# An attention and gated-FFN block on one core: half-row FFN tiles, two down banks, two work banks, and scores kept in PSUM

## Time and profile before

| | |
|---|---|
| median of 3 runs | 1118.66 us (1116.5 to 1118.77) |
| the profiled execution's own time | 1114.17 us |
| its span | 1112.0 us |
| PE, DVE, ACT, POOL busy | 84%, 80%, 54%, 63% |
| mean granted TensorE clock | 0.943 of full |

### The profile page before, as it was taken

The page is one execution under the profiler, slowest core; times in us unless marked ns, Lnnn a source line. Parts: engine busy times, 40 slices in busy tenths (PEclk is TensorE's granted clock), DMA queues, the critical chain, the costliest instruction groups (busy, mean ns, idle before and its releaser), DMA issues.

```text
span 1112.0 us, 13901 instructions
## 1 busy us (share of the span) xinstructions
PE 932.1 (84%) x4423; PEld 511.2 (46%) x4423; DVE 890.0 (80%) x1135; ACT 603.9 (54%) x907; POOL 697.9 (63%) x497
## 2 busy tenths in 40 slices
PE   5633538999889988999899988999899979889995
PEld 4432424555445544554445545454455543434442
DVE  4999997899798988899789988899889989642213
ACT  2546646655385646756475747655565635523422
POOL 2556555777479755876578756976487757632422
PEclk9856869999899999999999999999999999999997
DMA  6000310004002300023002400122002300230101
GB/s 163 22 17 3 97 37 16 16 23 115 1 1 76 95 20 0 22 73 94 0 0 75 113 0 0 48 81 59 1 1 76 77 0 1 76 76 1 38 1 38
DMA packets 78441, 45.93 MB, mean 41 GB/s; under 512 B 39616, under 2 KB 72384, under 8 KB 78400
## 3 DMA queue, kind: packets, MB, share of 16 engines
q1 hardware_dynamic: 73536, 45.10, 14.4%
q10 hardware_dynamic: 4864, 0.32, 0.3%
HBM read 28.63 MB, written 16.78 MB: 41 GB/s over the span
## 4 chain that ended last, share of the span: by engine, by line
PE 26%; DVE 26%; issue 17%; POOL 16%; ACT 13%; POOLq 0%; DVEq 0%; ACTq 0%
DVE prod L1088 10%; PE ps_gate L632 8%; PE ps_up L632 5%; PE ps_acc L656 4%; POOL sum L929 4%; PE ps_w L597 3%; POOL flo L982 3%; POOL xl L900 2%; DVE probs L1097 2%; ACT xb L736 2%; POOL o L977 2%; DVE attn L1097 2%; DVE xlo L1214 1%; POOL frs L885 1%; DVE fuse L1221 1%
## 5 line engine op out<-in xcount | busy, mean ns | idle before, releaser
L1088 DVE TENSOR_TENSOR prod<-ps_x,qkvl 128x2048 f32<-128x2048 f32 x128 | 290.5, 2282 | 8.2 <-ACT ps_x L761 7.7
L632 PE MATMUL ps_gate<-xhi,wg 128*128 128x512 f16 x512 | 198.7, 388 | 21.4 <-DVE xlo L1214 12.0
L982 POOL TENSOR_TENSOR flo<-fuse,fhi 128x512 f16<-128x512 f32 x128 | 148.9, 1166 | 92.4 <-ACT fhi L829 92.2
L632 PE MATMUL ps_up<-xhi,wu 128*128 128x512 f16 x512 | 196.3, 383 | 8.7 <-DVE fuse L1221 8.7
L632 PE MATMUL ps_gate<-xlo,wg 128*128 128x512 f16 x512 | 198.9, 388 | 0.0
L920 POOL TENSOR_TENSOR sum<-prod 128x1024 f32<-128x1024 f32 x64 | 150.7, 2361 | 75.6 <-DVE prod L1088 54.7
L632 PE MATMUL ps_up<-xlo,wu 128*128 128x512 f16 x512 | 195.7, 382 | 0.0
L929 POOL TENSOR_TENSOR sum<-prod 128x1024 f32<-128x1024 f32 x64 | 151.3, 2369 | 67.3 <-DVE prod L1088 66.2
L823 ACT ACTIVATE gact<-ps_gate,sgate 128x512 f32<-128x512 f32 x128 | 87.5, 684 | 157.3 <-PE ps_gate L632 156.9
L1221 DVE SCALAR_TENSOR_TENSOR fuse<-ps_up,sup,gact 128x512 f32<-128x512 f32 x128 | 95.4, 746 | 95.1 <-PE ps_up L632 78.8
L597 PE MATMUL ps_w<-wqkvl,xt 128*128 128x256 f32 x448 | 123.6, 401 | 24.2 <-ACT xt L743 16.5
(11 more groups left out here) (168 smaller groups left out, 1451.5 us busy)
## 6 DMA issues: line engine op xcount, KB each, us to landing
xb<-in_L_attn_x SPq DMA_DIRECT2D x64, 128.0 KB, 2.7
xr<-in_L_attn_x SPq DMA_DIRECT2D x16, 512.0 KB
attn_rows<-ratt SPq DMA_DIRECT2D x16, 512.0 KB, 3.7
o<-attn_rows SPq DMA_DIRECT2D x32, 256.0 KB, 4.2
out_x<-o SPq DMA_DIRECT2D x14, 512.0 KB
x<-in_L_ffn_w_gate SPq DMA_DIRECT2D x1, 1024.0 KB, 5.5
xr<-in_L_ffn_w_up SPq DMA_DIRECT2D x1, 1024.0 KB, 8.3
out_x<-o SPq DMA_DIRECT2D x4, 256.0 KB
```

Source lines behind the costliest of these rows:

```text
L632: mm = nc.tensor.matmul(ps[:], w[:, k, :], xs[:, k, :], start=(k == 0 and part == 0), stop=(k == KB - 1 and part == 1))
L982: nc.gpsimd.tensor_tensor(flo[:, m % SPLITS, :], fuse[:, m % 2, :], fhi[:, m % SPLITS, :], ALU.subtract).then_inc(flo_done, 1)
L1088: nc.vector.tensor_tensor(prod[:, half].rearrange("p (s j k) -> p s j k", j=WIN, k=WIN), left[:, :, None, :].broadcast_to([P, 4 * WIN, WIN ...
```

## The change

- **FFN on halves of 256 rows.** The 16 steps `m` of a tile are now 2 halves of 8 (`CHUNKS`). A step covers two blocks of 128 hidden units for 256 rows: `gate` and `up` are 16 matmuls of 256 columns where they were 8 of 512; silu and `fuse` are two instructions of 256 columns each, as each block has its own scale. `down` is still 8 matmuls of 512 columns, into two banks. DVE reads the two banks after each half (`finish(t, hi)`), so twice a tile, with its own statistics; `y` is a tensor of its own of half the size.
- **The next tile's rows in halves.** `fx(t, hi, u)` transposes two column blocks of one half. Only half 0 stands ahead of the next tile's first `gate`.
- **No end of a tile.** The last three `down` and the last `fuse_hi`, `fuse_lo` of a tile stand among the next tile's first steps.
- **PSUM.** The two freed banks become a second work bank (`bank_of` says which a step uses) and a second `ps_x`, one for each branch. `qk_sum` writes the scores into `ps_x[br]`, softmax and exp work there in place, `probs` is gone.
- **A new order** in all four lists. `qx`, `exp` no longer wait for the other branch's products. The transfers are the same, and the weights in SBUF too.

```diff
-        ps_acc = [pb(f"ps_acc{q}") for q in range(NQ)]
-        ps_w = pb("ps_w")
-        ps_x = pb("ps_x")
+        ps_acc = [pb(f"ps_acc{q}") for q in range(2)]
+        ps_w = [pb(f"ps_w{i}") for i in range(2)]
+        ps_x = [pb(f"ps_x{br}") for br in range(2)]
...
+        def bank_of(step):
+
+            return {"ln1_fin": 0, "fx": step[-1], "xt": step[-1], "qkv": step[-1] % 2, "cat": step[-1],
+                    "proj": step[-1]}[step[0]]
+
         def body_steps(plan, last=False):
...
             for m in range(MB):
+                split = (0, m - 1) if m else (-1, MB - 1)
                 for i, part in enumerate(("gate", "up", "down")):
                     if part != "down":
                         steps.append((part, 0, m))
-                    elif m >= LAG:
-                        steps.append((part, 0, m - LAG))
-                    if part == "down":
+                    else:
+                        steps.append((part, 0, m - LAG) if m >= LAG else (part, -1, MB + m - LAG))
                         steps.append(("fuse", 0, m))
...
+                  (31, ("pv", b, 0)), (31, ("qkv", c, 0, 1)), (32, ("qkv", c, 0, 2)), (32, ("pv", b, 1)),
...
+            def gate_or_up(ps, m, w, done):
+                rows = slice(HALF * (m // CHUNKS), HALF * (m // CHUNKS) + HALF)
+                for i in range(2):
+                    j = 2 * (m % CHUNKS) + i
+                    for k in range(KB):
+                        for part, xs in enumerate((xhi, xlo)):
+                            mm = nc.tensor.matmul(ps[:, HALF * i:HALF * i + HALF], w[:, k, P * j:P * j + P], xs[:, k, rows],
+                                                  start=(k == 0 and part == 0), stop=(k == KB - 1 and part == 1))
                 mm.then_inc(done, 1)
...
             def down(t, m, bank):
                 pe.wait_ge(flo_done, MB * t + m + 1)
-                if m == 0:
-                    need(pe, acc_read, NQ * t)
...
+                if m % CHUNKS == 0:
+                    need(pe, acc_read, NQ * t + 2 * (m // CHUNKS))
+                for i in range(2):
+                    for part in range(2):
+                        for q in range(2):
+                            mm = down_part(m, part, i, q)
...
             def qk_sum(at, u, bank):
-                reduce_unit(at, u, 0, probs)
+                reduce_unit(at, u, 0, ps_x[u // 2][:, 256 * (u % 2):256 * (u % 2) + 256])
...
-                pr = probs[:, br].rearrange("p w i j -> p (w i) j")
+                pr = ps_x[br][:].rearrange("p (s j) -> p s j", j=WIN)
...
-                nc.vector.scalar_tensor_tensor(fuse[:, m % 2, :], ps_up[:], sup[:, m:m + 1], gact[:, m % 2, :],
-                                               ALU.mult, ALU.mult).then_inc(fuse_done, 1)
+                for i in range(2):
+                    part, j = slice(HALF * i, HALF * i + HALF), 2 * (m % CHUNKS) + i
+                    a = nc.vector.scalar_tensor_tensor(fuse[:, m % 2, part], ps_up[:, part], sup[:, j:j + 1],
+                                                       gact[:, m % 2, part], ALU.mult, ALU.mult)
+                a.then_inc(fuse_done, 1)
...
+            def finish(t, hi, bank):
+                dve.wait_ge(down_done, MB * t + CHUNKS * hi + CHUNKS)
+                need(dve, s_out, 16 * (2 * t + hi))
+                for q in range(2):
                     nc.vector.tensor_tensor(y[:, q, :], ps_acc[q][:], sdown[:], ALU.mult).then_inc(acc_read, 1)
```

More of the change, by code:

```diff
@@ L247, in need @@
                 eng.wait_ge(s, value)
-        WORK = ("xt", "qkv", "cat", "proj", "fx_transpose", "ln1_fin")
+        WORK = ("xt", "qkv", "cat", "proj", "fx", "ln1_fin")
         def released(step, t):
@@ L400, in walk, with run @@
         def walk(eng, todo):
-            last_use, turn = [None, None], [0]
-            def run(steps, tile, banks=1):
+            last_use = [None, None]
+            def run(steps, tile):
                 for step in steps:
@@ L627, in fx_transpose @@
                 mm.then_inc(fx_tr, 1)
-            def gate_or_up(ps, w, done):
-                for k in range(KB):
-                    for part, xs in enumerate((xhi, xlo)):
-                        mm = nc.tensor.matmul(ps[:], w[:, k, :], xs[:, k, :], start=(k == 0 and part == 0),
-                                              stop=(k == KB - 1 and part == 1))
+            def gate_or_up(ps, m, w, done):
[6 more added lines that the diff above has]
+                                                  start=(k == 0 and part == 0), stop=(k == KB - 1 and part == 1))
@@ L664, in down_last @@
                         pe.wait_ge(flo_done, MB * t + m + 1)
-                    for part, f in enumerate((fhi, flo)):
-                        mm = nc.tensor.matmul(ps_acc[q][:], f[:, m % SPLITS, P * q:P * q + P], wd[:, m, :],
-                                              start=False, stop=(m == MB - 1 and part == 1))
+                    for i in range(2):
+                        for part in range(2):
+                            mm = down_part(m, part, i, q)
                 mm.then_inc(last_down, 1)
@@ L691, in scale_spread @@
                 pe.wait_ge(top_pow2, 1)
[L692 removed]
+                nc.tensor.matmul(ps_up[:, 0:1], ones[:], top[0:1, 2:3], start=True, stop=True).then_inc(top_all, 1)
             pe.wait_ge(setup_pool, SETUP_POOL)
@@ L822, in gate @@
                 need(act, fuse_done, MB * t + m - 1)
-                nc.scalar.activation(gact[:, m % 2, :], ps_gate[:], ACT.Silu,
-                                     scale=sgate[:, m:m + 1]).then_inc(silu_done, 1)
+                for i in range(2):
+                    part, j = slice(HALF * i, HALF * i + HALF), 2 * (m % CHUNKS) + i
+                    a = nc.scalar.activation(gact[:, m % 2, part], ps_gate[:, part], ACT.Silu, scale=sgate[:, j:j + 1])
+                a.then_inc(silu_done, 1)
             def fuse_hi(t, m, bank):
```

372 lines of the change are left out of this document (177 added, 195 removed).

## The result

The median is 1010.9 us (1009.9 to 1014.05) against 1118.72 (1116.5 to 1118.89) for the kernel before, run beside it: a ratio of 0.9045, 95% interval 0.9022 to 0.9068. The profiled execution's own time is 1010.97 us, its span 1009.2. The forecast was 1062 with a range of 1033 to 1100: the sign was right, but the gain of 108 us is nearly twice the 57 forecast, and lies outside the range.

A forecast was written before the change was run, and what follows sets the result against it. PE (112.2 us busy per steady tile) and DVE (109.3) were taken as together close to the bound. Six tiles -43, last two -8, end -2, start -4 make -57: from 1118.66 to 1062 us, range 1033 to 1100.

The forecast's parts named there:

- the short matmuls: Gate and up matmuls of 256 columns: 0.109 us apart with loads hidden, +0.6 us per tile.
- the subtraction: Softmax subtraction on DVE with one input in PSUM: 0.69 us each, -2.7 us of DVE per tile.
- the turn: Passage between tiles: PE's 4.4 us of waits go, and with them the clock drop of 1.7 us per tile.
- start: Stretch ahead of the steady tiles: -4 us, with ends of +8 and -15.
- end: From the last matmul to the last addition: one row block left instead of two, -2 us.
- The down hand-over: `down` of step 8 waits until DVE has read both down banks: just fits, priced at +0.3 us per tile.
- The first: Rival at gate and up: weight load not hidden under 256-column matmuls, 1472 us if fully added; 5 in 100.
- third rival: Late hand-over of the two down banks, 15 times up to 4.5 us, 1130 us; 9 in 100.
- Sum per steady tile: Turn waits -4.4, clock -1.7, second work bank -2.0, short matmuls +0.6, down banks +0.3: -7.2 us per tile.
- the last two tiles: Last but one: half of 8.4 us `fuse` waits, 1.9 for `xlo` and a clock drop, -8 us; last tile: 0.
- fourth rival: Mid-tile waits go too and the period nears PE's 111 us: 1035 us; 8 in 100.
- second rival: DVE becomes the bound, staying at 91% busy, tile near 119.5 us: 1091 us in all; 20 in 100.

The follow-up runs named there:

- 5: Changed kernel's structure (half tiles, banks, carried `down`) under the four order lists of the kernel before, with steps renamed and some moved as needed: 1143.42 us.
- 2: Changed kernel with one work bank in place of two, and two neighbouring steps of the order swapped: 1181.83 us.
- 4: Changed kernel with one work bank and one `ps_x`, scores in SBUF, still in the new order and half tiles: 1258.63 us.
- 9: Kernel before with only the last three `down` and last split carried into the next tile, and the ending's `finish` three slots later: 1148.45 us.
- run 1: Changed kernel with the softmax scores in SBUF again, both `ps_x` banks kept: 1027.59 us.

## Why the prediction was wrong

*Right.* Its single prices: the short matmuls 0.109 apart (0.109), loads hidden; `fuse` +1.8 per tile (+2.0); the subtraction 0.699 (0.69), -2.7 in all; PSUM read as fast as SBUF (0.680 for the sum); the turn without waits and at full clock; start -2.8 (-4) and end -3.4 (-2). DVE's busy time is 107.5 (109.4); its terms came near their prices, and where the other 1.9 us went was not followed up. The down hand-over "just fits", by 0.3 to 0.5 us. The first and the third rival did not happen.

*Wrong: "Sum per steady tile: -4.4 - 1.7 - 2.0 + 0.6 + 0.3 = -7.2".* It is -13.0 in the tile shown, 80.2 for 43 over the six, and so misses 37 of the 46 us between the forecast and the two spans (the last two tiles miss another 8). In the tile shown the 5.8 missed have two parts.

- *Idle time of PE*, 3.6: forecast -6.1 (4.4 + 2.0 - 0.3), found -9.7 (10.8 to 1.15). This is the step that failed. The prediction took only the waits whose releaser the change touches by name (the turn, the work bank) and left 4.4 us of waits for `gact`, `catt`, `cent`, `xt` and the rest of the bank's in place, without a reason. The largest of them, of that tile of before:

```profile
PE ps_gate L632 <- ACT gact L823: 1.7, 2, 0.9
```

  In the new tile 1.0 us of waits is left in all. Such a wait is not the property of its releaser: it is the lack of other work ahead of it. With a second bank PE has something else to do there, and the new order puts it there. The runs bear this out from both sides. With all the memory and the old order (5) PE waits again for `xt` (1.4), `gact` (0.8) and `catt` (0.6); with the new order and one bank (2) for `xt`, `cent` and `catt` again, besides `qkvl` and `xlo`.
- *Busy time of PE*, 2.2: forecast -1.1 (the clock, -1.7, and +0.6), found -3.3. Worked out, not tested: a matmul's record is 0.38 long at a distance of 0.216, so in front of each idle piece 0.16 us of a modelled end counts as busy. The tile before has thirteen idle pieces, 2.1 us of such ends, that after it three, 0.5 us; this makes 1.6 of the 2.2, and the rest stays open. PE's "111 us" in the fourth rival, the floor, was thus some 2 too high.

*Wrong: the second rival's ceiling for DVE.* It held 20 in 100 that DVE stays at 91% busy. It is at 97.6%. The 13.7 idle us of before were waits, not a limit of the engine. Two lines of DVE's waits in the tile of before:

```profile
DVE xlo L1214 <- ACT xhi L798: 3.7, 3, 1.4
DVE ssum L1124 <- ACT ps_x L768: 3.5, 3, 2.3
```

Both chains now have other DVE work in them. What remains of DVE's idle time in 110 us is 1.7 in five pieces, the rest below 0.15 each.

*The last two tiles*: -8 by the waits for `fuse` in the last but one, found -16.4 by work. The prediction kept half of the 8.4 us for `fuse`; all that is left of PE's waits there, 817.6 to 1009, is:

```profile
PE ps_w L619 <- ACT o L795: 1.1, 1, 1.1
PE ps_gate L629 <- DVE xlo L1219: 0.4, 1, 0.4
```

*The fourth rival* (the waits in the middle go too, the period nears PE's work) is what happened, held at 8 in 100. It was priced at 1035, 24 us too high: 11 for the floor of the six tiles, 8 for the last two, and 5 for the profiled execution of before, which was under its median. The prediction called 10.8 us of idle time the gain at stake, and then had no reason from the profile why 4.4 of it should stay.

## What to carry to other kernels

When a change frees a buffer and rewrites the order too, the parts cannot be priced one by one from the waits of the profile before: here the three partial kernels that were tried on the way from before to after lost 3 to 13% (runs 4, 5 and 9), and the whole won 10. The bound to work from is the busy time of the two fullest engines, less the modelled ends: forecast between that and the sum of the named waits, and give the full bound a real chance where the lists are written by hand. A step that looks like a cost at one place (the `down` steps at the turn) may be the cover of another; ask of each moved step what it was hiding. And when two engines end at 98%, look for the third limit before taking work from either.

## What the runs showed of the hardware that was not expected

- The subtraction with both inputs in SBUF takes 1377 ns on average before and 1547 in run 1, for 699 with one input in PSUM, at the same size on the same engine. The mean hides two cases. With POOL idle the old form takes 0.69 us too; where POOL works on `sum`, `cent` or `flo` it ends 0.55 us behind POOL's operation, however long that takes: at 137.85 for POOL's end at 137.30, and after 2.35 us at 197.34 for `cent`'s end at 196.79. Lines of the kernel before:

```profile
81.19 0.69 DVE L1116 TENSOR_TENSOR probs<-probs,smax 128x512 f32<-128x512 f32 x1
...
134.95 2.35 POOL L929 TENSOR_TENSOR sum<-prod 128x1024 f32<-128x1024 f32 x1 [7.83 <-DVE prod L1088]
136.75 1.10 DVE L1116 TENSOR_TENSOR probs<-probs,smax 128x512 f32<-128x512 f32 x1
```

  The new form takes 0.70 with the same `cent` of POOL running beside it (449.33, POOL from 448.78 for 2.35). The Trainium skill ("SBUF — State Buffer", section "SBUF: two separate sides") describes a port pair that VectorE with two SBUF inputs and GpSimd take in turns, each for a whole instruction; these rows agree with it.
- Taking 1/16 of the gate and up matmuls out made two idle pieces of 1.5 to 2.6 us at the loop's turn on PE with no releaser in the profile, and 27 instruction packets inside the loop where the changed kernel has none. Fewer instructions in a loop's body are not always less time.
